# Two weight transfers moved from the sync engine's queue to ScalarE's, at the start of an octonion feed-forward kernel

## The reference

```
xn  = layernorm(x)
Wq  = scale * clip(round(W / scale), -1, 1),  scale = mean(|W|)       (for w_gate, w_up, w_down)
lin(v, W)[k, o] = sum over i, j, d of S[j, i, k] * v[i, d] * Wq[j, o, d]   (S: signs of the octonion product, 8 components)
h   = silu(lin(xn, w_gate)) * lin(xn, w_up)
out = x + autocorrelation_attention(xn) + lin(h, w_down)
```

## Time and profile before

| what | value |
|---|---|
| median of three runs | 554.21 us (553.62 to 554.5) |
| the profiled execution's own time | 553.78 us |
| its span | 552.0 us |
| PE busy in the span | 539.7 us, 98% |
| DVE, ACT, POOL busy | 472.3, 385.0, 466.7 us |
| DMA over the span | 36.65 MB, mean 66 GB/s |

### The profile page before, as it was taken

The page is one execution under the profiler, slowest core; times in us unless marked ns, Lnnn a source line. Parts: engine busy times, 40 slices in busy tenths (PEclk is TensorE's granted clock), DMA queues, the critical chain, the costliest instruction groups (busy, mean ns, idle before and its releaser), DMA issues.

```text
span 552.0 us, 16462 instructions
## 1 busy us (share of the span) xinstructions
PE 539.7 (98%) x6596; PEld 507.2 (92%) x6596; DVE 472.3 (86%) x1227; ACT 385.0 (70%) x622; POOL 466.7 (85%) x337
## 2 busy tenths in 40 slices
PE   6999999999999999999999999999999999999997
PEld 5899998899998999999999999999999999998997
DVE  4987999898888879988998979987998979984965
ACT  4879889976947589665977589766967575646432
POOL 3506739998999998999989998999989999999950
PEclk9999999999999999999999999999999999999999
DMA  9820212013220042201330042201330021302122
GB/s 207 193 78 1 77 27 82 8 38 110 79 88 17 3 153 66 66 1 39 137 100 12 1 152 67 65 4 44 130 99 12 3 77 35 95 3 71 33 87 97
DMA packets 26996, 36.65 MB, mean 66 GB/s; under 512 B 13686, under 2 KB 20774, under 8 KB 26918
## 3 DMA queue, kind: packets, MB, share of 16 engines
q1 hardware_dynamic: 26918, 35.58, 21.8%
HBM read 21.23 MB, written 8.39 MB: 54 GB/s over the span
## 4 chain that ended last, share of the span: by engine, by line
PE 70%; POOL 13%; issue 9%; DVE 4%; DMA 2%; ACT 2%; SPq 0%; POOLq 0%; ACTq 0%; DVEq 0%
PE acc L659 17%; PE acc L495 14%; PE acc L488 13%; PE acc L505 10%; PE acc L649 6%; PE acc L544 4%; POOL hop L1988 3%; POOL hs L1981 3%; POOL hs L1976 3%; POOL hs L1980 3%; PE acc L518 2%; DMA hop<-in_w_gate 2%; PE acc L561 2%; POOL hop L1985 1%; POOL hs L1975 1%
## 5 line engine op out<-in xcount | busy, mean ns | idle before, releaser
L659 PE MATMUL acc<-wd,hop 128*128 128x128 f16 x1920 | 112.7, 219 | 0.8 <-DVE acc L1441 0.4
L659 PEld LDWEIGHTS acc<-wd,hop 128*128 128x128 f16 x1920 | 109.4, 98 | 1.7 <-DVE acc L1441 0.9
L947 ACT ACTIVATE pk<-acc 128x512 f32<-128x512 f32 (+1 forms) x120 | 65.9, 556 | 64.0 <-PE acc L488 26.2
L1988 POOL TENSOR_TENSOR hop<-hs,hop 128x1024 f16<-128x1024 f32 (+1 forms) x46 | 98.2, 2135 | 9.0 <-ACT hop L1025 8.8
L1985 POOL TENSOR_TENSOR hop<-hx,hop 128x1024 f16<-128x1024 f32 (+1 forms) x46 | 98.3, 2137 | 5.3 <-ACT hop L1015 5.3
L505 PE MATMUL acc<-wl,xop 128*128 128x172 f16 x1024 | 84.2, 237 | 1.1 <-DVE acc L1459 0.9
L505 PEld LDWEIGHTS acc<-wl,xop 128*128 128x128 f16 x1024 | 77.6, 97 | 3.2 <-DVE acc L1459 1.1
L1975 POOL TENSOR_TENSOR hs<-hx 128x512 f32<-128x512 f32 (+1 forms) x47 | 60.2, 1281 | 15.3 <-DVE hx L1540 11.7
L1423 DVE TENSOR_TENSOR bd<-acc,pk 128x256 f32<-128x256 f32 (+1 forms) x104 | 41.0, 394 | 30.0 <-ACT pk L947 29.6
L1025 ACT ACTIVATE hop<-hs 128x1024 f16<-128x1024 f32 (+1 forms) x46 | 48.4, 1053 | 23.8 <-POOL hs L1981 23.7
L1980 POOL TENSOR_TENSOR hs<-hs 128x512 f32<-128x512 f32 (+1 forms) x47 | 59.8, 1273 | 3.7
(11 more groups left out here) (206 smaller groups left out, 1164.2 us busy)
## 6 DMA issues: line engine op xcount, KB each, us to landing
xr<-in_x SPq DMA_DIRECT2D x16, 512.0 KB, 4.4
zx<-in_x SPq DMA_DIRECT2D x16, 512.0 KB, 3.6
out_y<-zx SPq DMA_DIRECT2D x15, 512.0 KB, 2.6
hop<-hop SPq DMA_DIRECT2D x40, 84.0 KB
hop<-hop SPq DMA_DIRECT2D x96, 21.0 KB
hop<-in_w_gate SPq DMA_DIRECT2D x2, 480.0 KB, 9.6
hop<-in_w_up SPq DMA_DIRECT2D x1, 960.0 KB
hop<-in_w_down SPq DMA_DIRECT2D x1, 960.0 KB, 17.3
```

The costliest lines, as they stand in the source:

```text
L659: last = nc.tensor.matmul(dst, operand(g, c, t, form, level), wd[0:WIDE[c], slot, c, :], start=which == 0 and c == order[0] and s // 2 not ...
L947: nc.scalar.activation(pk[:, q % 2, :, 0:wide], pair[:, :, T:T + wide], ACT.Copy, scale=XS if u[0] == "X" else 1.0).then_inc(copied, 1)
L1988: nc.gpsimd.tensor_tensor(half_of(g, c, NJ + 4 * Y, 1), by_tile(hs[rows, 0:4, :]), half_of(g, c, NJ + 4 * Y, 0), ALU.subtract).then_inc(h_ ...
```

## The change

The transfers of gate's second half (components 4 to 7) are no longer issued by the sync engine. ScalarE issues them as the first instructions of its list: the pairs at once, then a wait for `row_zero` >= 1, then the threes. They signal the same semaphore `gate_rest`. The two transfers go into the queue of ScalarE, which is another than the sync engine's. Nothing else is changed; no engine's use of the data moves in its list.

```diff
@@ sync engine
-            first, rest, every = slice(0, NJ // 2), slice(NJ // 2, NJ), slice(0, NJ)
+            first, every = slice(0, NJ // 2), slice(0, NJ)
             pairs_of_units(0, w_gate, first, w_in[0])
             sp.wait_ge(row_zero, 1)
             threes_of_units(0, w_gate, first, w_in[0])
             last_units(0, w_gate)
-            pairs_of_units(0, w_gate, rest, gate_rest)
-            threes_of_units(0, w_gate, rest, gate_rest)
             sp.wait_ge(row_zero, 2)
             last_units(1, w_up)
@@ ScalarE
+            rest = slice(NJ // 2, NJ)
+            nc.scalar.dma_start(up_stage[0][THIRDS:P, rest, 0:2, :],
+                                w_gate[rest, SPLIT:SPLIT + 2 * (P - THIRDS), :].rearrange("j (p c) d -> p j c d", c=2)).then_inc(gate_rest, 16)
+            act.wait_ge(row_zero, 1)
+            nc.scalar.dma_start(up_stage[0][0:THIRDS, rest, :, :], w_gate[rest, 0:SPLIT, :].rearrange("j (p c) d -> p j c d", c=NC)).then_inc(gate_rest, 16)
             act.wait_ge(const_done, 2)
             nc.scalar.activation(junk[:, 0:1], ones[:, 0:1], ACT.Silu).then_inc(table_in, 1)
```

## The result

The changed kernel took 557.6 us (median of 6 runs, 556.59 to 558.57) against 554.32 us for the kernel before, run beside it (6 runs). The ratio is 1.0059, 95% interval 1.0046 to 1.0071: slower by 0.59%, 3.3 us. The forecast was 555.7 with a range to 557.2; the direction was right, and the time lies above the range.

What follows compares the result with a forecast made beforehand. Bound: about 17 us before TensorE's first product, set by gate's transfer on full DMA engines, then a nearly gapless product stream. The late first half adds 1.5 us: 554.21 + 1.5 = 555.7 us, range 554.2 to 557.2.

Steps and rivals of the forecast that it cites:

- The late first half: Before the first product: gate's first half lands last, usable at 12.2 instead of 10.13 us, delaying everything after by 1.5 us.
- t: Start of ScalarE's first sum, when gate's first half can be used; forecast 12.2 us, 10.13 before.
- t - 10.7: Shift of everything after VectorE's x_low for a first sum starting at t; +1.5 us forecast.
- the 2.45 MB: Bytes moved when all of gate is there, the first half landing last; forecast reached at 10.3 us.
- the lag: Time from a byte amount being reached to its data being usable; mean of gate's two halves 1.9 us.
- x_low - t: Time from ScalarE's first sum to VectorE's x_low, worked out from durations before as near 4.4 us.
- rival (3): TensorE slows down after a longer gap ahead of the gate transposes: +1.6 us on top, 557.3 us; chance 0.09.
- strict alternation: DMA engines alternate between both queues, so x's 16 descriptors take 12 pairs and 4 threes of gate's rest, 0.295 MB.
- (1): Total DMA rate doesn't rise: t = 13.1 to 13.7, shift 2.4 to 3.0, time 556.9 us; chance 0.22.
- (2): Two queues mix well, 1.10 MB of gate at 320 GB/s: t = 11.0, shift +0.3, 554.5 us; chance 0.22.
- (4): Not slower: sync engine's queue served first, rest fills gaps and lands earlier; gain at most 0.65 us, 553.55; chance 0.07.
- Costs put at nothing: ScalarE's list start: two issues and a wait delay its table load, covered before x lands; 1.5 us without cover.

Runs made afterwards that it cites:

- e1: The changed kernel with 56 instead of 32 idle transposes ahead of TensorE's wait for gate's first half; 556.29 us, ratio 1.0030.
- e6: The changed kernel with gate's last units issued right behind x and up's behind up's threes; ratio 1.0028, profiled run 555.21 us, the others 556.51 to 556.94.
- e4: The kernel before, one queue, with gate's rest issued ahead of its first half and 64 instead of 32 idle transposes; 556.97 us, ratio 1.0040.
- e12: The changed kernel with ScalarE waiting for row_zero >= 2 ahead of both issues, which come at 2.70 and 3.13 us; 554.61 us, ratio 1.0008.
- e2: The changed kernel with engines taking gate's rest before its first half, and gate's last units on ScalarE's queue; 555.21 us, ratio 1.0004.
- e8: The kernel before with 8 instead of 32 idle transposes at the start, no transfer changed; 556.01 us, ratio 1.0019.
- e3: The kernel before with gate's first half and last units issued by ScalarE first, the rest left in the sync engine's queue; 558.26 us, ratio 1.0051.
- e11: The changed kernel with ScalarE's two issues moved behind its warm-up activation, to about 3.7 us; 562.32 us, ratio 1.0138.
- e10: The kernel before, but ScalarE issues the first half's threes and the rest's pairs as its first instructions; 553.59 us, ratio 0.9977.
- e9: The kernel before, but ScalarE issues the first half's threes and the rest's pairs after its warm-up activation; 560.27 us, ratio 1.0100.

## Why the prediction was wrong in size

**The late first half: right.** The step said t = 12.2 and a shift of t - 10.7. Measured t was 12.51, which gives +1.8: the 2.45 MB were reached near 10.6 us by the window table, where 10.3 was forecast, and the lag was the 1.9 taken. x_low - t was 4.38, 4.39 and 4.37 in kernels whose clock stayed up (e1 and e6, e4, e12), against the 4.4 worked out. The second sum stood behind the first without waiting for a DMA, as forecast. e2 shows it from the other side: with the lists in the order of landing the cost is gone.

**The clock: the step that failed.** The prediction put TensorE's fall to the lower level as rival (3), priced at +1.6 "on top of the forecast", and gave it 0.09. It happened in all six runs. Its price was somewhat too high: 1.26 us in the profile (5.64 less 4.38), since the first four transposes still ran at full speed; 1.3 to 1.7 between runs of e6, 0.6 to 1.6 in e8. The sum with it is 1.8 + 1.26 = 3.06 for the 3.03 seen at x_low, and 3.3 timed. Taking the forecast's own t and this rival's own price would have given 554.21 + 1.5 + 1.6 = 557.3. The mistake was the chance, and that a case that goes with the forecast was treated as an alternative to it. The pause itself was 2.27 us, shorter than the 3.5 forecast, because the 32 idle transposes ran at the low speed to their end (6.68 us instead of 5.18). That is no effect of the change that can be shown: the same 32 took 5.33 to 6.58 us in the other profiles. The length of the pause alone did not decide: the clock fell after 2.27 us here and stayed after 3.42 us in e6's profile. What decides is open. The 1.00 that rival (3) read beside its 390 ns says nothing of the clock there: the trace has no clock record before 6.6 us, and the table reads 1.00 where it has none.

**How two queues share: wrong in the way, about right in the result.** The prediction took a strict alternation, with x's 16 descriptors carrying 16 of the rest's. In fact the rest's pairs went beside x's first tile, its threes only after x. The amounts nearly cancel: x's second tile was used at 6.98 where 6.85 was forecast, and gate moved faster afterwards (326 GB/s from 5 to 8 us, not 237) but ended in a slow stretch. The Trainium skill ("DMA: Bandwidth & Descriptors", section "Queues, rings and completion order") has each DMA engine going round its queues packet by packet; e3's even split, 159 to 151 packets, agrees for that stretch, and e11 shows that it doesn't tell when a queue's transfer starts.

**Rivals (1), (2), (4).** (1), no rise of the rate, is refuted for single stretches by 326, 279 and 284 GB/s. But over the first 13 us the changed kernel moved 2.83 MB against 2.77, and t came in below its 13.1 only by 0.6. The Trainium skill ("DMA: Bandwidth & Descriptors", section "Issuing engines are not separate DMA queues") has issuing from several engines save only issue time. The changed kernel agrees, since it gained nothing; e10 does not quite, since it gained 0.23% and moved 2.98 MB in the same 13 us. (2) had the rate for the middle stretch (320) but not the slow end. (4) is out: the order of landing did change.

**Costs put at nothing.** The table load moved from 0.72 to 2.07 and ended at 3.35; x came later than that, and nothing waited. Right.

**Open.** What makes the slow stretches (172 GB/s at 8 to 10 us before, 157 at 10 to 13 after) is not settled: moving the last units did not remove them. The changed kernel's slow stretch is up's pairs: 214 of the 226 data packets that start from 11 to 13 us have their 1024 bytes, and these took about 160 ns each, where the rest's pairs had taken about 50 beside x. That is a coincidence in time and not a tested cause. Why mixed transfers move faster was not isolated: pairs and threes write different partitions, but e10 changed more than that. Two queues alone don't do it: by 13 us the four profiled kernels with one queue had moved 2.75 to 2.77 MB, e10 2.98 and e12 3.11, but e3 2.70 and e11 2.51.

## What to carry to other kernels

When a transfer is moved to another engine's queue, work out its place in the order of all issues, by time, and then the order of landing against the order in which each engine's fixed list uses the data; a piece that lands early gains nothing if the piece ahead of it in the lists lands late for it. A rival that follows from the forecast itself (a longer pause, then a slower TensorE) belongs in the sum, not beside it; a change that makes a pause longer should carry the price of the slower clock with a real chance. If two queues are used, split so that the halves still land in order, and issue both parts together, as e10 did; the gain here was 0.6 to 1.9 us of 554.7.

## What the runs showed of the hardware

- In the changed kernel and in e9 to e12 the transfers of the two queues start in the order of their issues, across the queues: issued at 3.75 us the rest had 18 of its 544 packets under way by 10 us and was usable at 19.6 (e11); issued at 2.7 the two halves were used at 11.51 and 13.48 (e12). While two are under way they often share about evenly (159 to 151 packets in e3 from 8.5 to 10.5 us), but not always (272 to 154 in e10 from 6 to 8 us).
- The granted clock doesn't follow from the length of TensorE's pause alone: it fell after a pause of 2.27 us that 6.68 us of slow transposes preceded (changed kernel), and stayed in one run of six of e6 after a pause of 3.42 us. In e6's other five runs, the same program, it fell (mean clock 0.997).
- The trace's clock records begin some way into the span (at 6.6 us in the kernel before, at 15.4 in e8). Ahead of the first record the table reads 1.00 although equal transposes took 390 to 421 ns there and 273 later; such durations tell the level.
